# A transformer block with block-quantised FFN weights: the weight pipeline divided one weight further ahead, with seven raw buffers and three split buffers

## What is computed

```python
def block_qdq_weight(w, block=32, bits=4):          # w_gate, w_up, w_down: 1376 x 512 (down: 512 x 1376)
    wb = w.reshape(out_f, in_f // block, block)
    scale = max(max(abs(wb), -1) / 7, 1e-12)
    return (clip(round(wb / scale), -8, 7) * scale).reshape(out_f, in_f)
def act_qdq(x):                                       # 16 bits, over the whole tensor
    mn, mx = min(min(x), 0), max(max(x), 0)
    scale = max((mx - mn) / 65535, 1e-12); zp = clip(round(-mn / scale), 0, 65535)
    return (clip(round(x / scale) + zp, 0, 65535) - zp) * scale
xq   = act_qdq(layernorm(x))
up   = act_qdq(xq @ wu.T)
gate = act_qdq(xq @ wg.T)
gate = act_qdq(gate * fixed_qdq(sigmoid(gate)))
x    = x + act_qdq(gate * up) @ wd.T
```

## Time and profile before

| | |
|---|---|
| median of 3 runs | 826.1 us (825.26 to 829.15) |
| the profiled execution | 826.9 us, span 825.1 us |
| PE busy | 709.1 us (86%) |
| DVE busy | 645.9 us (78%) |
| POOL busy | 528.8 us (64%) |
| ACT busy | 516.8 us (63%) |
| mean granted TensorE clock | 0.943 |

### The profile page before, as it was taken

How to read it: one execution, slowest core, us unless ns; L and a number is a source line. 1 busy time by engine, 2 the same in 40 slices (tenths; PEclk the granted TensorE clock), 3 DMA queues, 4 the chain that set the end, 5 groups by cost and what they waited for, 6 DMA issues and landing times.

```text
span 825.1 us, 12740 instructions
## 1 busy us (share of the span) xinstructions
PE 709.1 (86%) x3310; PEld 326.0 (40%) x3311; DVE 645.9 (78%) x1332; ACT 516.8 (63%) x968; POOL 528.8 (64%) x498
## 2 busy tenths in 40 slices
PE   0597989663195997999999999999999688999998
PEld 0243434221032443444444444444444253444443
DVE  6886768878699587888888988888888767656655
ACT  4567757659466446777777777777776543655540
POOL 1897768937376456888788888888884414344330
PEclk9899989975598998999999999999999999999998
DMA  8315665523335236677666666666645612232311
GB/s 321 102 65 121 134 154 118 126 63 76 65 64 128 76 102 134 166 182 183 154 145 132 137 146 143 145 144 143 144 94 102 103 39 86 105 114 78 114 38 51
DMA packets 199348, 97.72 MB, mean 118 GB/s; under 512 B 188929, under 2 KB 189185, under 8 KB 196370
## 3 DMA queue, kind: packets, MB, share of 16 engines
q1 hardware_dynamic: 199314, 97.32, 48.5%
HBM read 49.85 MB, written 1.05 MB: 62 GB/s over the span
## 4 chain that ended last, share of the span: by engine, by line
PE 64%; POOL 10%; DVE 10%; issue 5%; DMA 5%; ACT 4%; SPq 1%; DVEq 0%; ACTq 0%; POOLq 0%
PE ps L998 21%; PE ps L999 20%; PE ps L1000 20%; ACT arena L692 2%; DMA arena<-arena 2%; POOL arena L483 2%; POOL arena L504 2%; DVE arena L1319 2%; DMA arena<-in_ctx_t 2%; DVE arena L1313 2%; DVE arena L1316 2%; PE ps L1164 1%; POOL arena L496 1%; POOL arena L479 1%; POOL arena L473 1%
## 5 line engine op out<-in xcount | busy, mean ns | idle before, releaser
L998 PE MATMUL ps<-arena 128*128 128x512 f16 (+2 forms) x996 | 385.9, 388 | 48.0 <-ACT arena L692 17.7
L999 PE MATMUL ps<-arena 128*128 128x512 f16 (+2 forms) x996 | 385.4, 387 | 0.0
L1000 PE MATMUL ps<-arena 128*128 128x512 f16 (+2 forms) x996 | 384.1, 386 | 0.0
L692 ACT ACTIVATE arena<-arena 128x512 f16<-128x512 f32 (+8 forms) x425 | 279.6, 688 | 99.7 <-POOL arena L649 29.5
L998 PEld LDWEIGHTS ps<-arena 128*128 128x128 f16 (+1 forms) x996 | 99.5, 100 | 175.9 <-issue 55.0
L1000 PEld LDWEIGHTS ps<-arena 128*128 128x128 f16 (+1 forms) x996 | 99.7, 100 | 122.4 <-issue 11.1
L1313 DVE TENSOR_TENSOR arena<-arena 128x512 f16<-128x512 f32 (+1 forms) x169 | 127.7, 786 | 25.0 <-ACT arena L692 24.2
L999 PEld LDWEIGHTS ps<-arena 128*128 128x128 f16 (+1 forms) x996 | 99.4, 100 | 113.0 <-issue 8.4
L649 POOL TENSOR_SCALAR arena<-arena,rden 128x512 f32<-128x512 f32 x128 | 115.0, 898 | 24.2 <-DVE rden L1664 15.0
L1319 DVE SCALAR_TENSOR_TENSOR arena<-ps,arena 128x512 f32<-128x512 f32 (+1 forms) x149 | 100.4, 706 | 15.3 <-ACT arena L692 7.9
L894 ACT ACTIVATE arena<-arena,mneg 128x512 f32<-128x512 f32 x124 | 88.8, 716 | 35.6 <-DVE mneg L1644 35.6
(11 more groups left out here) (125 smaller groups left out, 665.7 us busy)
## 6 DMA issues: line engine op xcount, KB each, us to landing
arena<-in_moe_w SPq DMA_DIRECT2D x18, 768.0 KB, 4.4
arena<-in_ffn_w SPq DMA_DIRECT2D x33, 256.0 KB, 2.8
arena<-in_wq SPq DMA_DIRECT2D x8, 1024.0 KB, 5.2
arena<-in_wo SPq DMA_DIRECT2D x8, 1024.0 KB, 5.0
arena<-in_kv_w SPq DMA_DIRECT2D x4, 1024.0 KB, 4.8
arena<-arena SPq DMA_TRANSPOSE x177, 3.2
arena<-in_ctx SPq DMA_DIRECT2D x1, 2048.0 KB, 9.1
arena<-in_ctx_t SPq DMA_DIRECT2D x1, 2048.0 KB, 13.5
```

What stands on the lines that cost most here:

```text
L692: return a.activation(out_, in_, ACT.Copy, scale=scale, bias=bias)
L998: pe.matmul(out_, lhs[0], rhs[0], start=first, stop=False)
L999: pe.matmul(out_, lhs[0], rhs[1], start=False, stop=False)
L1000: return pe.matmul(out_, lhs[1], rhs[0], start=False, stop=last)
```

## The change

The raw buffers become seven and their loads alternate between two semaphores, so that two are on their way. The buffers of dequantised and of split weights become three, in place of four; the memory is moved about for it. `divide` and `round_weights` go one weight further ahead of `scale_back` and `weight_high`: POOL's turn n divides n + 5 and ACT's turn n rounds n + 4, with weight 3 divided and rounded ahead of the turns. DVE looks seven ahead, does `between()` ahead of `weight_low`, and makes the pair's scales in even turns.

```diff
-RAW = 5
-DQ = 4
+RAW = 7
+DQ = 3
-SC = 6
+SC = 8
-        wt = carve(56, (DQ, 2 * D), F16)
-        deq = carve(64, (DQ, D))
+        deq = carve(60, (DQ, D))
+        wt = carve(66, (DQ, 2 * D), F16)
-        raw = carve(194, (RAW, D))
+        raws = [carve(194 + 2 * i if i < 5 else 46 + 2 * i, (D,)) for i in range(RAW)]
 # SP
             def ring(n):
-                if not isinstance(n, int) or n >= 1:
-                    sp_wait(in_raw, n * 16)
-                if not isinstance(n, int) or n >= RAW:
-                    sp_wait(w_deq, n - RAW + 1)
-                sp.dma_start(one(raw, n % RAW), one(ffn_w, n)).then_inc(in_raw, 16)
+                if n >= 2:
+                    sp.wait_ge(in_raw[n % 2], 16 * (n // 2))
+                if n >= RAW:
+                    sp.wait_ge(w_deq, n - RAW + 1)
+                sp.dma_start(raws[n % RAW], ffn_w[:, n]).then_inc(in_raw[n % 2], 16)
 # POOL, weights(n)
-                if n + 4 < NCH:
-                    divide(n + 4)
+                if n + 5 < NCH:
+                    divide(n + 5)
...
             v_low(4)
+            divide(3)
             v_low(5)
             v_low(6)
             scale_back(2)
             for u in range(MT - 1, MT + 1):
                 v_low(u)
-            divide(3)
+            divide(4)
 # ACT
             weight_high(1)
+            round_weights(3)
             v_out(MT - 1)
...
             def tile_turn(n, dst):
                 weight_high(n + 2)
-                round_weights(n + 3)
+                if n + 4 < NCH:
+                    round_weights(n + 4)
                 tile_out(n, dst)
...
-                if i < FT - 3:
-                    round_weights(2 * FT + i + 3)
+                if i < FT - 4:
+                    round_weights(2 * FT + i + 4)
 # DVE
             def weights(n, between=None):
-                if n + 6 < NCH:
-                    block_maxima(n + 6)
+                if n + 7 < NCH:
+                    block_maxima(n + 7)
+                if between:
+                    between()
                 if n + 2 < NCH and low_owner(n + 2) == 1:
                     weight_low(n + 2)
-                if between:
-                    between()
-                if n + 6 < NCH and (n % 2 or n + 6 == NCH - 1):
-                    pair_scales(n + 6)
+                if n + 7 < NCH and (n % 2 == 0 or n + 7 == NCH - 1):
+                    pair_scales(n + 7)
...
             pair_scales(5)
+            block_maxima(6)
             with_tiles(0, up_after)
```

More of the change, by code:

```diff
@@ L261, in block_kernel @@
         in_x, in_par, in_ctx, in_ctt = sem("in_x"), sem("in_par"), sem("in_ctx"), sem("in_ctt")
-        in_raw, in_kw, in_mask, in_aq, in_ao = sem("in_raw"), sem("in_kw"), sem("in_mask"), sem("in_aq"), sem("in_ao")
+        in_raw, in_kw, in_mask, in_aq, in_ao = [sem("in_raw0"), sem("in_raw1")], sem("in_kw"), sem("in_mask"), sem("in_aq"), sem("in_ao")
         in_me, in_mp, stored = sem("in_me"), sem("in_mp"), sem("stored")
@@ L353, in _ @@
             kw_load(2)
-            for n in range(2):
-                turn_w(n)
-                ring(n + RAW + 1)
-            for n in range(2, NCH):
+            for n in range(NCH):
                 turn_w(n)
@@ L493, in divide @@
                 g.wait_ge(w_inv, n // 2 + 1)
-                v = one(raw, n % RAW).rearrange("p (a b) -> p a b", b=QB)
+                v = raws[n % RAW].rearrange("p (a b) -> p a b", b=QB)
                 s = one(dsi, n % SC).unsqueeze(2).broadcast_to([P, D // QB, QB])
@@ L728, in round_weights @@
             def round_weights(n):
-                w = one(raw, n % RAW)
+                w = raws[n % RAW]
                 a.wait_ge(w_div, n + 1)
@@ L1343, in block_maxima @@
             def block_maxima(n):
-                v.wait_ge(in_raw, 16 * (n + 1))
-                src = one(raw, n % RAW).rearrange("p (a b) -> p a b", b=QB)
+                v.wait_ge(in_raw[n % 2], 16 * (n // 2 + 1))
+                src = raws[n % RAW].rearrange("p (a b) -> p a b", b=QB)
                 return own.mark(v.tensor_reduce(one(dsc, n % SC), src, AX.X, ALU.max, apply_absolute_value=True))
```

## The result

The changed kernel takes 820.55 us (median of 6 runs, 818.34 to 821.45), the kernel before 826.15 us on the same chip (6 runs, 824.32 to 829.15). The ratio is 0.992, with a 95% interval of 0.9899 to 0.9941: faster by 5.6 us or 0.7%. That is inside the forecast range (811 to 823), 3.6 us above the 817 predicted. The profiled execution gained 6.9 us: 819.95 us with a span of 818.2, against 826.9 with 825.1. That is 1.3 us more than the medians gained, since the profiled execution before lay 0.75 us over its median and the one after 0.6 us under.

A forecast was written before the change was run, and what follows sets the result against it. PE bounds 380 to 630 us; earlier, gains must come from five PE pauses, with POOL bounding the gate stage. 0.8 + 1.8 + 1.3 + 3.6 + 2.5 = 10.0 us off 826.9 gives 816.9, as 817; range 811 to 823.

The forecast's parts named there:

- first link of the gating stage: DVE's low half at 204.49 us; ahead of it ACT's waits for `k_low` and `divide` go, together 2.1 us.
- 1 and 2, the up stage: PE's pauses for weight 3 and for the extrema of up shrink: gains 0.8 and 1.8 us.
- term 2: Extrema of up: a pair moves into DVE's wait, 1.2 us, plus 0.6 for shorter operations; gain 1.8 us.
- 3, the clock: After the extrema of up, a shorter pause may keep PE's clock up from 116 to 120 us; gain 1.3 us.
- term 4: Gate stage: POOL bounds, weight 20 comes 0.5 us earlier, DVE's tail loses extrema and scales; gain 3.6 us.
- 5, the gating stage: Its closing chain from DVE's low half to `turn_k(0)` and the product shortens; gain 2.5 us, bounds 0.6 and 4.0.
- The slower rival: Last gate turns and down turns: three buffers make `weight_high` wait for transpositions; about 836 us, chance 5%.
- The eaten lead: Gating stage: POOL's waits fill with work and DVE's operations lengthen; 6.3 us come back, 823.2 us, chance 20%.
- the case of more: POOL's lead from the up stage carries the gate stage, shrinking the 3.74 us pause too; about 811 us, chance 8%.

The follow-up runs named there:

- both moves: Changed kernel with POOL's four key low halves behind the gate's last weight and the first two key transpositions ahead of the last weights' ones: 810.83 us, ratio 0.9809.
- extrema first: Kernel before with only DVE's between() moved ahead of weight_low: 824.0 us against 825.82, ratio 0.9981.
- everything but the lead: Changed kernel with divide (n + 4) and rounding (n + 3) one weight less far ahead, as before: 821.12 us, ratio 0.9949.
- GpSimd relieved: Changed kernel with POOL's four low halves of the key weights (5.5 us) put behind the gate's last weight: 819.32 us, ratio 0.991.
- one load: Changed kernel where each weight load waits for the one before it, instead of two on their way: 819.07 us, ratio 0.9892.
- the kernel before with GpSimd relieved: Kernel before with POOL's four low halves of the key weights put behind the gate's last weight: 826.1 us, ratio 0.9993.
- keys early: First two key transpositions issued ahead of the last weights': changed kernel 813.39 us, same with divide and rounding one less ahead 816.9, kernel before 821.03.
- buffers alone: Kernel before with seven raw buffers, three dequantised and split ones, new layout and two loads on their way, nothing else: 826.84 us, ratio 1.0008.

## Why the prediction was right, and where it wasn't

The sign and the places were right; the sum, 10.0 us, was 3.1 too large against the 6.9 of the profiled execution, and 4.4 against the 5.6 of the medians. The mechanism held whole only in the gate's tail and in the first link of the gating stage; the clock's term came out in size for a reason that isn't the one given, which is luck. Term by term:

**1 and 2, the up stage: 2.6 expected, 1.4 measured.** Both signs were as forecast: weight 3's pause fell by 0.95 (0.8 expected; "1.4 us or less" held at 1.22), and the pause for the extrema to 1.48 ("under 1.5"), by 1.2 us for the 1.8 expected. The step that fails in term 2 is the 0.6 us added because low half and scales "are shorter where POOL isn't beside them": the scales take 1.13 us there, and 0.81 before. And the first tile starts at 70.42, 0.7 us later than before, which the prediction had only as a lower bound, for a load. What came is the lengthening for which it says "I count nothing": the first tile's two low halves now have a `scale_back` beside them. DVE, changed kernel:

```profile
65.86 1.85 DVE L1313 TENSOR_TENSOR arena<-arena 128x512 f16<-128x512 f32 x2
...
108.74 1.13 DVE L1316 TENSOR_SCALAR dsc<-dsc 128x32 f32<-128x32 f32 x1
```

The two low halves took 1.28 us together before and take 1.85, in five of the six kernels with the lead; in the sixth (both moves) and in the two without the lead they take 1.28. The first tile's start also scatters, from 69.5 to 70.5 us in five executions with the old lists at that place and from 70.2 to 71.7 us in eight with the new ones, so the 0.7 is good to about half a us.

The order of the extrema isn't the whole reason either. From the first tile to the extrema of up, in the executions that kept the clock there, it is 43.9 to 44.5 us with the old lists (three kernels), 43.55 with the extrema first, 43.70 and 43.72 with everything but the lead, and 41.8 to 42.4 with the whole of the up stage's change (three kernels). With the low half put first again it is 42.43 and the pause 1.43 us: once the lead is there, the order is worth nothing in this stage that can be told from a scatter of half a us. The prediction gave the lead no term of its own in this stage; it is worth 1.3 us or more of this stretch, part of which the later start takes back.

**3, the clock: 1.3 expected, 1.7 granted, but not for the reason given.** Summed over 2 us windows from 112 to 122 us, 1 minus the granted clock comes to 3.4 us before and 1.7 us after. (The prediction counted the 4 us at 0.50 of the earlier trace rows; the slow stretch was longer.) The step "a shorter pause may keep it up" fails: with pauses of 1.2 to 1.5 us at the extrema the clock fell in four kernels (among them the changed one, 1.48 us, and the one with GpSimd relieved, 1.19), and held at 1.00 in the one with extrema first (1.49), with one load and with both moves. Nor does the smaller loss need a shorter pause: the kernel before with GpSimd relieved has the old pause, 2.68 us, and loses 1.7 us. The gate front goes with this loss: 39.65 to 40.32 us in the three executions that lost 3.4 us, 38.49 to 38.87 in the five that lost 1.7 and weren't relieved of POOL's work, 37.68 (extrema first) and 36.94 (one load) where none was lost. So most or all of the front's 1.16 us is the clock's, and the 0.5 us that term 4 expected of weight 20 isn't shown.

**4, the gate stage: 3.6 expected, and with term 3 4.9; measured 4.1.** The mechanism was right: POOL at 10.00, the pause still there, the tail shorter by DVE's moved work. The tail gave 2.96 for 3.6. PE's last wait is 4.91 us ("4 to 5"). The extrema's part was sized at 2.3 us and gave 1.7 alone and 1.4 beside the scales' edit; the scales' part was sized at 1.3 and gave 1.6 and 1.2. About what is missing stands as a wait: the last low half now waits 1.60 us for ACT, and 1.00 before:

```profile
158.31 0.86 DVE L1313 TENSOR_TENSOR arena<-arena 128x512 f16<-128x512 f32 x1 [1.60 <-ACT arena L690]
...
163.04 0.17 DVE L1429 TENSOR_REDUCE ext<-mm 128x2 f32<-128x22 f32 x1
```

and in the kernel before:

```profile
160.88 0.86 DVE L1313 TENSOR_TENSOR arena<-arena 128x512 f16<-128x512 f32 x1 [1.00 <-ACT arena L692]
```

"POOL is the bound" was half the truth: relieving it of 5.5 us brought 1.0 us.

**5, the gating stage: 2.5 expected, 1.5 measured.** The first link came about as forecast: ACT's wait of 1.04 us for `k_low` is gone (no wait at 194.78), and from one `k_high` to the next it is 8.60 and 7.66 us where it was 9.28 and 8.66, so 1.7 of "together 2.1" arrived. The step that fails is the second one, "`least` no longer stands between the low half and `k_mean`, 0.6 us": the last `k_high` now waits 1.78 us, 1.40 before, because POOL's `k_pow` waits 1.55 us for DVE's `k_mean`, and that stands behind a low half that waits for ACT in turn. The extrema's order in the kernel before changes nothing in this stage (53.94 against 53.91), the buffers neither (53.92), the lead on top of the rest gives 2.1 us, and the change without its lead makes the stage 0.5 to 0.6 us longer, with the keys late and with the keys early (54.48 against 53.91, 49.02 against 48.52). The cause of that last 0.6 wasn't found; what is left for it are the scales in even turns and the maxima seven ahead, which no run had alone.

**Loads, three buffers: nothing expected, nothing measured** (826.84 against 825.82 us, interval about 1). The slower rival fell with it. **Everything behind 223 us** is shifted: 602.4 and 602.5 us. The matmuls of the first gate tile take 0.61 us and not the 0.38 by which a kept clock was to be seen.

**The eaten lead** happened in part. By form, 60 to 165 us (busy us, mean ns), before:

```profile
L504 POOL TENSOR_TENSOR arena<-arena,dsc 128x512 f32<-128x512 f32 x24 | 26.8, 1119 | 9.7 <-ACT arena L692 9.6
...
L1313 DVE TENSOR_TENSOR arena<-arena 128x512 f16<-128x512 f32 x19 | 16.1, 851 | 12.5 <-ACT arena L692 12.3
L1316 DVE TENSOR_SCALAR arena<-arena,aqp 128x512 int32<-128x512 f32 x9 | 9.6, 1071 | 0.0
L1316 DVE TENSOR_SCALAR dsc<-dsc 128x32 f32<-128x32 f32 x12 | 7.0, 586 | 0.2
```

and after:

```profile
L501 POOL TENSOR_TENSOR arena<-arena,dsc 128x512 f32<-128x512 f32 x24 | 29.3, 1220 | 1.6 <-ACT arena L690 1.6
...
L1313 DVE TENSOR_TENSOR arena<-arena 128x512 f16<-128x512 f32 x19 | 18.3, 965 | 13.8 <-ACT arena L690 13.8
L1316 DVE TENSOR_SCALAR dsc<-dsc 128x32 f32<-128x32 f32 x12 | 10.1, 845 | 0.1
L1316 DVE TENSOR_SCALAR arena<-arena,aqp 128x512 int32<-128x512 f32 x11 | 8.4, 766 | 0.0
```

Of `scale_back`'s 8.1 us of waits saved in this stretch, 3.7 us came back as waits of `v_low` for ACT, as the prediction argued against the case of more ("the lead ends there"), and 2.5 us as longer instructions. DVE's low halves and scales took 5.3 us more. This agrees with the Trainium skill (SBUF — State Buffer, section "SBUF: two separate sides"), by which one of the two engines blocks while the other holds the shared ports. Not every operation got longer: the quantised `up` was 305 ns shorter each, and DVE's reductions (L1419, L1420) took 0.67 us each in both kernels. No run took the sharing alone away, so its price in the total stays open; the run that differs from the change by the lead alone says that the lead still pays in the gating stage.

**Keys.** The prediction named ACT's 6.61 us for `turn_k(0)` as a link of the chain and took it as given. It was the largest item of the stage, and the experiment on it gained 5.5 us, in either kernel.

## What to carry to other kernels

In a ring of engines that each run their own list, ask of each stage which engine's tail ends it, and move out of that tail whatever isn't its own work: 2.96 of 6.9 us came from two moved groups of instructions. Waits of 15 us that disappear are no gain by themselves; here they were worth 2 us in the gating stage, where a short chain to another engine stood behind them, and about 1 us in the up stage. Read the issuing queue's order along the critical chain too: two transpositions issued earlier gave as much as seven buffers, a new order and a lead together.

## What the runs showed that was not expected

- **The slow stretch of PE's clock wanders.** In the gate's front and ahead of it, the granted clock falls below 1.00 at about 70 us (one load), at 80 us (both moves), at 112 us (changed), at 70 and again at 114 us (buffers alone) or not at all (extrema first), with the same lists around it or nearly so. Where it falls, 1 minus the clock comes to 1.7 us or 3.4 us over the 2 us windows. A kernel that is 2.4 us late at one border and whose next stage is 1.6 us shorter (one load) shows mostly this, and little of the edit. A second slow stretch, of 1.7 us, follows the pause for weight 20 in ten of the thirteen kernels, the changed one and the one before among them, so the tails compared above lie alike; it is missing in the kernel before with GpSimd relieved, in the kernel before with the keys early and in the one with both moves. In the kernel before the tail is as long without it (14.90, keys early) as with it (14.89). With both moves it is 10.67 against 11.79 us with GpSimd relieved alone, and whether that 1.1 us is the clock's isn't shown. What decides where it falls wasn't found.
- **A small instruction is lengthened as much as a large one.** The scales' 128x32 TENSOR_SCALAR takes 0.16 or 0.17 us at its fastest and 1.13 us at its slowest, in both kernels; what changed is how often, so that its mean rose from 586 to 845 ns. POOL's 128x512 `scale_back` takes 1.04 or 1.05 us in most cases, 1.2 to 1.5 in others, and once 2.03 in each of the two kernels.
- **The same edit gives the same gain whatever it is added to**, once read by stage: 5.39 us (kernel before) and 5.49 us (changed) for the keys, 2.07 us (keys late) and 2.10 us (keys early) for the lead, where the medians (0.6 us and 3.5 us for the lead) say little.
